# Attention from normalised rows: joined weights, and slice sums that are projected afterwards

## The chip, the cores and the metric

The kernel runs on one core of a Trainium2 chip. The metric is device time in microseconds (us) of one execution; the time before is the median of three timed runs. A trace of one further, profiled execution gives all times of single instructions.

## The reference

The input is x, 4 images of 32 x 32 tokens with 128 channels. Three stages follow one another: a deformable convolution on group-normalised x, an attention over 32 learned slices for each of 8 heads, and a mixture of 8 experts (top 2). The change touches the attention alone:

```
def _L1_attn_ref(x, W_x, b_x, W_slice, b_slice, W_temp, b_temp, W_out, b_out):   # x: layer-normalised tokens
    x_proj = (x @ W_x.T + b_x).reshape(B, N, H, D).transpose(0, 2, 1, 3)         # B 4, N 1024, H 8, D 32
    adaptive_temp = BASE_TEMP + jnp.clip(x_proj @ W_temp.T + b_temp, -0.4, 0.4)
    slice_logits = x_proj @ W_slice.T + b_slice - log_neg_log_eps
    slice_weights = jax.nn.softmax(slice_logits / adaptive_temp, axis=2)         # over the tokens
    slice_norm = slice_weights.sum(axis=2)
    eidetic = jnp.einsum('bhnc,bhng->bhgc', x_proj, slice_weights)
    eidetic = eidetic / (slice_norm + 1e-05)[..., None]
    out_x = jnp.einsum('bhgc,bhng->bhnc', eidetic, slice_weights)
    return out_x.transpose(0, 2, 1, 3).reshape(B, N, H * D) @ W_out.T + b_out
```

## The kernel before

All arithmetic is in float32. The work of the convolution sets the beat: each of the 4 images has 8 groups of 10 slots, so 80 slots an image, and each engine runs one long program, slot after slot. In a slot TensorE makes one part of the products of interpolation weights (`products`, L872); behind slot 0 of each group it contracts the previous group's products with the values (`contract`, L888) and projects an older one (`project`, L896). VectorE makes distances and ramps (L1574, L1588) and copies products out of PSUM in even slots (`take`, L1597); ScalarE makes edges and ramps (L1259, L1265), copies products in most odd slots (`lift`, L1283) and copies the contraction's result (L1274); GpSimd weighs (L752, L763). `contract` waits until the products of all ten slots have been copied. All queues are in order, so an instruction that waits holds up all that stands behind it on its engine.

Attention, routing and the experts of image b are woven into the slots of the images behind it: `side(b, slot)` runs, ahead of a slot's own products, the steps that the tables `PE_STEPS`, `ACT_STEPS` and `DVE_STEPS` give for that slot, for image b-1, and for image b-2 those 80 slots later. The three woven images 0, 1 and 2 share PSUM banks 6 and 7 and one set of buffers, so that a step waits until the one before it has been copied out. The last image, 3, goes through the same steps in a tail behind the convolution, three slots ahead, with banks of its own; between its steps stand the expert tiles of image 2 (`tile`, L1124 and L1136, with a gelu on ScalarE, L1350), also by slot. GpSimd gathers the experts' rows of images 0 and 1 with 16 indirect transfers (L734) in slots 9 to 20 of the convolution two images later; VectorE adds them (`add_rows`, L1847) in slots 21 to 25.

The attention of one image, with the slots of before: the normalised rows are transposed (`turn_tn`, 9) and copied (`tnT`). They are projected twice: channels by tokens (`xpT0`, `xpT1`, 10 and 11; ScalarE adds the bias while copying, L1297) and tokens by channels (`xp0`, `xp1`, 13 and 15; VectorE adds the bias, L1647). The temperatures are a product of the former (`temps`, 12; VectorE clamps them, L1637 and L1639, and takes reciprocals in two halves, L1641 and L1643). Four steps `logits0` to `logits3` (18 to 21) make a block-diagonal product (L1024), spread the reciprocals over the heads' rows (L1025), add the bias on ScalarE (L1305) and multiply on VectorE (L1656); `max0`, `max1` and `exp0`, `exp1` follow for each half. The weights are transposed (`turn_e0`, `turn_e1`, 23 and 25) and copied (`e0`, `e1`, L1312), the sums over tokens taken against the second projection (`sums`, 26, L1042), masked (`bdE`, L1673), multiplied by the output weights (`M`, 27) and applied (`out`, 28, L1055).

## Time and profile before

| what | us |
|---|---|
| median of 3 timed runs | 1352.8 |
| lowest and highest | 1348.93, 1356.17 |
| the profiled execution | 1359.09 |
| its span, first to last instruction | 1357.0 |
| TensorE, VectorE, ScalarE, GpSimd busy | 1027.2, 834.3, 786.9, 676.2 |
| mean granted TensorE clock, as a share of full speed | 0.878 |

The busy times are those of the profiled execution. They overlap, and each is spread over three parts of the span: a short preparation, the convolution with the work woven into it (from about 53 to 1150 us), and the tail.

### The profile page before, as it was taken

The page shows a single profiled execution, that of the slowest core. Times are in us where ns is not written, and L with a number is a line of the kernel's source. Part 1 is how long each engine was busy: PE and PEld are TensorE (multiplying, and loading weights), DVE is VectorE, ACT ScalarE, POOL GpSimd, SP SyncE. Part 2 cuts the span into 40 slices and gives each one's busy share as a digit, 9 for nine tenths or more (in the row PEclk, how much of TensorE's full clock was granted, in tenths as well). Part 3 has the DMA queues.
Part 4 walks back from the last instruction along what each step waited for, and adds up shares of the span by engine and source line. Part 5 has one row for each costly group of instructions (what it writes and reads, how often), then busy time and mean ns, then how long its engine had stood idle before and what let it go on. Part 6 is the DMA issues. An engine that isn't in the chain of part 4 may idle for free.

```text
span 1357.0 us, 51003 instructions
## 1 busy us (share of the span) xinstructions
PE 1027.2 (76%) x22444; PEld 838.1 (62%) x22444; DVE 834.3 (61%) x1632; ACT 786.9 (58%) x1435; POOL 676.2 (50%) x640
## 2 busy tenths in 40 slices
PE   4576877886887758998787758988777678768790
PEld 3455655565566646886576647875566466558690
DVE  5767766676648846556678645566678474535361
ACT  2786756765667644667567545766675542354460
POOL 2664545554535593435745764437655852002334
PEclk9697987978989778999998778999997789886995
DMA  7302121311000322552110323632113120523612
GB/s 163 100 24 54 65 54 48 71 44 45 23 23 24 91 70 72 164 163 59 46 38 24 103 81 85 190 102 57 39 37 89 45 68 25 165 78 93 193 54 75
DMA packets 140445, 103.26 MB, mean 76 GB/s; under 512 B 43529, under 2 KB 123714, under 8 KB 139714
## 3 DMA queue, kind: packets, MB, share of 16 engines
q1 hardware_dynamic: 136130, 91.61, 24.5%
q0 software_dynamic: 4096, 8.40, 2.1%
q8 instruction: 179, 2.93, 0.9%
q14 instruction: 40, 0.33, 0.1%
HBM read 76.31 MB, written 23.66 MB: 74 GB/s over the span
## 4 chain that ended last, share of the span: by engine, by line
PE 55%; ACT 19%; DVE 14%; issue 7%; DMA 2%; POOL 1%; SPq 1%; DVEq 0%; POOLq 0%; ACTq 0%
PE ps L888 13%; PE ps L872 10%; ACT xsb L1265 7%; PE ps L1124 6%; PE ps L896 6%; PE ps L1136 5%; DVE asb L1597 3%; ACT asb L1283 2%; ACT xsb L1259 2%; DMA ring<-in_L_ffn_W 2%; DVE region L1820 2%; PE ps L845 2%; DVE xsb L1574 2%; PE ps L1042 1%; DVE ysb L1588 1%
## 5 line engine op out<-in xcount | busy, mean ns | idle before, releaser
L763 POOL TENSOR_TENSOR ysb<-ysb,rw 128x576 f32<-128x576 f32 x300 | 336.8, 1145 | 366.5 <-DVE ysb L1588 366.3
L872 PE MATMUL ps<-xsb,ysb 64*64 64x96 f32 x11008 | 331.1, 272 | 111.0 <-DVE asb L1597 27.0
L872 PEld LDWEIGHTS ps<-xsb,ysb 64*64 64x64 f32 x11008 | 281.6, 151 | 174.0 <-issue 78.5
L1265 ACT ACTIVATE xsb<-xsb,pick 128x576 f32<-128x576 f32 (+1 forms) x480 | 336.2, 750 | 5.2
L1597 DVE COPY asb<-ps 128x960 f32<-128x960 f32 (+1 forms) x208 | 215.7, 1043 | 112.3 <-PE ps L888 100.0
L752 POOL TENSOR_TENSOR ysb<-rw,count 128x576 f32<-128x576 f32 (+1 forms) x150 | 174.3, 1162 | 78.3 <-PE ps L872 77.4
L888 PE MATMUL ps<-asb,vd 32*32 32x258 f32 x8192 | 183.0, 388 | 18.8 <-issue 16.6
L1274 ACT ACTIVATE osp<-ps 128x258 f32<-128x258 f32 x128 | 43.0, 443 | 254.2 <-PE ps L888 254.2
L1350 ACT ACTIVATE region<-ps,b_col 128x128 f32<-128x128 f32 x368 | 105.3, 370 | 103.6 <-PE ps L1124 101.8
L888 PEld LDWEIGHTS ps<-asb,vd 32*32 32x32 f32 x8192 | 121.5, 103 | 69.1 <-issue 35.9
L1574 DVE TENSOR_TENSOR xsb<-rw,ps 128x576 f32<-128x576 f32 (+1 forms) x150 | 108.4, 722 | 60.8 <-PE ps L872 59.9
L1588 DVE SCALAR_TENSOR_TENSOR ysb<-ysb,ps 128x576 f32<-128x576 f32 (+1 forms) x158 | 113.7, 719 | 20.1 <-POOL ysb L752 20.1
L724 POOL DMA_INDIRECT sorted_rows<-region,row_no x64 | 63.5, 993 | 122.1 <-DVE row_no L1785 105.5
L1259 ACT ACTIVATE xsb<-xsb 128x576 f32<-128x576 f32 (+1 forms) x160 | 105.3, 658 | 23.5 <-DVE xsb L1574 23.5
L1124 PE MATMUL ps<-region,ring 128*128 128x128 f32 x552 | 88.1, 308 | 26.8 <-ACT region L1350 11.2
L1283 ACT ACTIVATE asb<-ps 128x768 f32<-128x768 f32 x112 | 93.8, 837 | 24.9 <-PE ps L872 24.7
L1124 PEld LDWEIGHTS ps<-region,ring 128*128 128x128 f32 x552 | 75.8, 212 | 38.4 <-issue 22.9
L734 POOL DMA_INDIRECT picked<-expert_rows,row_no x64 | 63.1, 986 | 59.3 <-DMA expert_rows<-xsb 24.6
L896 PE MATMUL ps<-outw,osp 128*128 128x128 f32 x512 | 78.6, 317 | 11.9 <-issue 7.8
L1606 DVE TENSOR_TENSOR x_tok<-x_tok,ps 128x1024 f32<-128x1024 f32 x32 | 39.0, 1218 | 75.0 <-PE ps L896 71.7
L896 PEld LDWEIGHTS ps<-outw,osp 128*128 128x128 f32 x512 | 72.5, 226 | 17.6 <-issue 14.0
L1136 PE MATMUL ps<-ring,region 128*128 128x128 f32 x552 | 78.2, 288 | 6.0 <-ACT region L1350 4.0
(270 smaller groups left out, 1220.2 us busy)
## 6 DMA issues: line engine op xcount, KB each, us to landing
ring<-in_L_ffn_W SPq DMA_DIRECT2D x138, 256.0 KB, 3.2
vd<-group_values SPq DMA_DIRECT2D x128, 128.0 KB, 2.7
set_rows<-ring SPq DMA_DIRECT2D x4, 1376.0 KB, 6.6
rw<-set_rows SPq DMA_DIRECT2D x30, 172.0 KB, 3.4
group_values<-region SPq DMA_DIRECT2D x32, 128.0 KB, 3.6
asb<-in_L_ffn_W SPq DMA_DIRECT2D x16, 256.0 KB, 4.8
region<-sorted_rows SPq DMA_DIRECT2D x6, 512.0 KB, 4.9
expert_rows<-region SPq DMA_DIRECT2D x6, 512.0 KB, 5.3
```

What stands on the lines that cost most here:

```text
L752: pl.tensor_tensor(ysb[:, ch % DEPTH, 0:sets, NU - 1, :], rows_of(ig)[:, 1, first:first + sets].rearrange("p (s o) -> p s o", o=1) .broadc ...
L763: pl.tensor_tensor(ysb[:, ch % DEPTH, 0:sets, u, :], ysb[:, ch % DEPTH, 0:sets, NU - 1, :], rows_of(ig)[:, 2 + u, first:first + sets].rear ...
L872: last = pe.matmul(ps[64 * j:64 * j + 64, bank + i, NV * GRID * q:NV * GRID * (q + 1)], ysb[rows, ch % DEPTH, col, :, :].rearrange("p u y ...
L888: last = pe.matmul(ps[32 * jc:32 * jc + 32, j, 0:NI * AM], vd[rows, ig % 2, x, :], asb[rows, x, :, :].rearrange("p i n -> p (i n)"), start ...
L896: last = pe.matmul(pcol(project_bank(ig), t), osp[:, ig % 2, t // 4, t // 2 % 2, t % 2 * P:(t % 2 + 1) * P], outw[:, ig % G, :], start=Tru ...
L1124: last = pe.matmul(ps[:, hidden_bank(b, i), j * P:(j + 1) * P], ring_part(b, i, 0)[:, j * P:(j + 1) * P], turned_rows(b, i), start=True, s ...
L1136: last = pe.matmul(ps[:, expert_bank(b, i), 0:C], hT[:, i % 2, j, :], ring_part(b, i, 1)[:, j * P:(j + 1) * P], start=(j == 0), stop=(j == ...
L1259: act.activation(away, away, ACT.Relu, bias=1.0, scale=-1.0).then_inc(s.x_within, 1)
L1265: act.activation(xsb[:, ch % DEPTH, 0:sets, v, :], xsb[:, ch % DEPTH, 0:sets, NV - 1, :], ACT.Relu, bias=pick[:, v:v + 1], scale=-1.0).the ...
L1574: dve.tensor_tensor(xsb[:, ch % DEPTH, 0:sets, NV - 1, :], rows_of(ig)[:, 0, first:first + sets].rearrange("p (s o) -> p s o", o=1) .broad ...
L1588: dve.scalar_tensor_tensor(v, v, 0.0, units.rearrange("p (o q) -> p o q", o=1) .broadcast_to([P, sets, GRID]), ALU.max, ALU.min).then_inc( ...
L1597: dve.tensor_copy(asb[:, :, :, first:first + m].rearrange("p x i m -> p i x m"), ps[:, bank:bank + 2, 0:GRID * m].rearrange("p i (m x) -> ...
```

## The change

The two projections of the rows fall away. In their place two products of weights are made once, in slot 12 of image 0's convolution (`join_weights`): `wc`, the projection times the block-diagonal slice weights, and `wtc`, the projection times the temperature weights; the biases are carried through likewise. Temperatures and logits are taken from the transposed normalised rows `tnT` with these. The sums are taken of the normalised rows themselves (all 256 columns against 128 channels), copied to SBUF by ScalarE, and projected afterwards in a new step `eid`; the bias enters there as `bx_b` times a diagonal matrix of the sums of weights, which VectorE makes (`diagonal`). The tables of steps are renumbered: `temps` from 12 to 11, `logits0` to `logits3` from 18 to 21 to 16 to 19, the transposes from 23 and 25 to 21 and 23, `sums` to 25, `eid` at 26; `M` and all that follows stay where they were. The diff's core, first TensorE, then ScalarE (`join_weights`, `sums`), then VectorE (`xp0` to `bdE`):

```
+PE_STEPS = {9: ("turn_tn",), 11: ("temps",), 16: ("logits0",), 17: ("logits1",), 18: ("logits2",), 19: ("logits3",),
+            21: ("turn_e0",), 23: ("turn_e1",), 25: ("sums",), 26: ("eid",), 27: ("M",), 28: ("out",),
...
             def join_weights():
+                pe.wait_ge(s.setup_done, 1)
+                pe.wait_ge(s.turned_copied, 2)
+                pe.wait_ge(s.ln_cols_copied, 4)
+                temp_columns = wt_bd.rearrange("p (m f) -> p m f", f=HG)[:, :, 0]
+                for h in range(2):
+                    pe.matmul(ps[:, 6, h * P:(h + 1) * P], wx_raw[:, h, :], ws_bd, start=True, stop=True)
+                for h in range(2):
+                    pe.matmul(ps[:, 6, 2 * P + h * DH:2 * P + (h + 1) * DH], wx_raw[:, h, :], temp_columns,
+                              start=True, stop=True)
+                pe.matmul(ps[:, 7, 0:2], ws_bd, bx_col[:, :], start=True, stop=True)
+                for i in range(4):
+                    last = pe.matmul(ps[32 * i:32 * i + 32, 7, 2:3], temp_columns, bx_col[:, i // 2:i // 2 + 1],
+                                     start=True, stop=True)
+                last.then_inc(s.weights_joined, 1)
...
-                elif step in ("xpT0", "xpT1"):
...
+                elif step == "temps":
                     pe.wait_ge(s.tnT_copied, b + 1)
-                    for c in range(2):
-                        last = pe.matmul(ps[:, bank_of(b, 1 + h) + c, :], wxT[:, h * P:(h + 1) * P],
-                                         tnT[:, c * 512:(c + 1) * 512], start=True, stop=True)
...
+                        last = pe.matmul(ps[32 * i:32 * i + 32, bank_of(b, 3), :], wtc[:, h * DH:(h + 1) * DH],
+                                         tnT[:, c * 512:(c + 1) * 512], start=True, stop=True)
                     last.then_inc(s.temps_summed, 1)
-                elif step in ("xp0", "xp1"):
...
-                    pe.matmul(ps[:, bank, :], ws_bd[:, :], xpT[:, h, c * 512:(c + 1) * 512], start=True, stop=True)
+                    pe.matmul(ps[:, bank, :], wc[:, h * P:(h + 1) * P], tnT[:, c * 512:(c + 1) * 512],
+                              start=True, stop=True)
...
                 elif step == "sums":
                     pe.wait_ge(s.e_copied, 2 * b + 2)
+                    for t in range(NT):
+                        last = pe.matmul(ps[:, bank_of(b, 12), 0:2 * P], tn_tok[:, t, :], own(b).e_tok[:, t, :],
+                                         start=(t == 0), stop=(t == NT - 1))
+                    last.then_inc(s.slice_sums, 1)
+                elif step == "eid":
+                    pe.wait_ge(s.diagonal_made, b + 1)
+                    pe.wait_ge(s.sums_copied, b + 1)
                     for h in range(2):
-                        for t in range(NT):
-                            last = pe.matmul(ps[:, bank_of(b, 12), h * P:(h + 1) * P], own(b).xp_tok[:, t, h * P:(h + 1) * P],
-                                             own(b).e_tok[:, t, h * P:(h + 1) * P], start=(t == 0), stop=(t == NT - 1))
-                    last.then_inc(s.slice_sums, 1)
+                        both = ps[:, bank_of(b, 12) + 1, h * P:(h + 1) * P]
+                        pe.matmul(both, bx_b[:, h * P:(h + 1) * P], own(b).diagonal[:, h, :], start=True, stop=False)
+                        last = pe.matmul(both, wxT[:, h * P:(h + 1) * P], own(b).sums[:, h, :], start=False, stop=True)
+                    last.then_inc(s.eid_summed, 1)
...
+            def join_weights():
+                act.wait_ge(s.weights_joined, 1)
+                act.activation(wc[:, :], ps[:, 6, 0:2 * P], ACT.Copy).then_inc(s.joined_copied, 1)
+                act.activation(wtc[:, :], ps[:, 6, 2 * P:2 * P + 2 * DH], ACT.Copy).then_inc(s.joined_copied, 1)
...
+                elif step == "sums":
+                    act.wait_ge(s.slice_sums, b + 1)
+                    act.activation(own(b).sums, ps[:, bank_of(b, 12), 0:2 * P].rearrange("p (h n) -> p h n", h=2),
+                                   ACT.Copy).then_inc(s.sums_copied, 1)
...
-                elif step in ("xp0", "xp1"):
...
+                elif step == "diagonal":
+                    dve.wait_ge(s.exp_done, 2 * b + 2)
+                    for h in range(2):
+                        last = dve.tensor_scalar(own(b).diagonal[:, h, :], ident[:, :], a_sum[:, h:h + 1], None, ALU.mult)
+                    last.then_inc(s.diagonal_made, 1)
...
                 elif step == "bdE":
-                    dve.wait_ge(s.slice_sums, b + 1)
+                    dve.wait_ge(s.eid_summed, b + 1)
```

How this stands on TensorE for the first woven image, from slot 9 to slot 19. In these rows L872 (after: L892) are products, L888 (L908) the contraction, L986 and L1005 before the two projections, L993 (L1005) the temperatures, L1024 and L1025 (L1018 and L1020) one step of the logits. Before:

```order
L978 MATMUL ps<-ident,region 128x128 x8
L872 MATMUL ps<-xsb,ysb 64x96 x16
L986 MATMUL ps<-region,wxT 128x512 x2
L872 MATMUL ps<-xsb,ysb 64x96 x20
L888 MATMUL ps<-asb,vd 32x258 x128
L986 MATMUL ps<-region,wxT 128x512 x2
L872 MATMUL ps<-xsb,ysb 64x96 x16
L993 MATMUL ps<-region,wt_bd 32x512 x4
L872 MATMUL ps<-xsb,ysb 64x96 x20
L1005 MATMUL ps<-wxT,region 128x256 x4
L872 MATMUL ps<-xsb,ysb 64x96 x36
L1005 MATMUL ps<-wxT,region 128x256 x4
```

And after, the same stretch:

```order
L999 MATMUL ps<-ident,region 128x128 x8
L892 MATMUL ps<-xsb,ysb 64x96 x36
L908 MATMUL ps<-asb,vd 32x258 x128
L1005 MATMUL ps<-region,wtc 32x512 x4
L892 MATMUL ps<-xsb,ysb 64x96 x88
L1018 MATMUL ps<-region,wc 128x512
L1020 MATMUL ps<-region,head_pick 128x512
L892 MATMUL ps<-xsb,ysb 64x96 x16
L1018 MATMUL ps<-region,wc 128x512
L1020 MATMUL ps<-region,head_pick 128x512
```

Nothing stands between the products of slots 9 and 10 and the contraction any more, the temperatures come right behind the contraction, and the logits start in slot 16 with only products between.

On ScalarE, around slot 19 of the same image: L1305 (after: L1309) adds the logits' bias, L1341 (L1349) is the exponential with its table load, L1283 (L1292) `lift`, L1274 before the copy of the contraction's result, L1265 (L1274) ramps. Before:

```order
L1283 ACTIVATE asb<-ps 128x2x32x12
L1305 ACTIVATE region<-ps,bslice_col 128x512
L1259 ACTIVATE xsb<-xsb 128x18x32
L1265 ACTIVATE xsb<-xsb,pick 128x18x32
L1274 ACTIVATE osp<-ps 128x2x43x3 x4
L1305 ACTIVATE region<-ps,bslice_col 128x512
L1341 ACT_TABLE_LOAD
L1341 ACTIVATE region,a_sum<-region,a_nmax 128x1024
```

And after:

```order
L1309 ACTIVATE region<-ps,bslice_col 128x512
L1349 ACT_TABLE_LOAD
L1349 ACTIVATE region,a_sum<-region,a_nmax 128x1024
L1274 ACTIVATE xsb<-xsb,pick 128x18x32 x2
L1292 ACTIVATE asb<-ps 128x2x32x12
L1268 ACTIVATE xsb<-xsb 128x18x32
L1274 ACTIVATE xsb<-xsb,pick 128x18x32
L1283 ACTIVATE osp<-ps 128x2x43x3 x4
```

The first exponential stood behind the contraction of slot 20 and the copy of its result; it now stands ahead of the copy of slot 19's products, for which that contraction waits.

In the tail, on TensorE, L1124 and L1136 (after: L1126 and L1138) are the expert tiles of image 2 between the steps of image 3; L1036 (L1031) are the transposed weights, L1042 (L1036) the sums, L1048 (L1050) is M. Before:

```order
L1036 MATMUL ps<-ident,xsb 128x128 x16
L1124 MATMUL ps<-region,ring 128x128 x4
L1136 MATMUL ps<-ring,region 128x128 x4
L1042 MATMUL ps<-xsb 128x128 x16
L1048 MATMUL ps<-woutT,ysb 128x128 x2
```

And after:

```order
L1031 MATMUL ps<-ident,xsb 128x128 x8
L1126 MATMUL ps<-region,ring 128x128 x4
L1138 MATMUL ps<-ring,region 128x128 x4
L1031 MATMUL ps<-ident,xsb 128x128 x8
L1036 MATMUL ps<-xsb,region 128x256 x8
L1126 MATMUL ps<-region,ring 128x128 x4
L1138 MATMUL ps<-ring,region 128x128 x4
L1044 MATMUL ps<-ysb,bx_b 128x128
L1045 MATMUL ps<-ysb,wxT 128x128
L1044 MATMUL ps<-ysb,bx_b 128x128
L1045 MATMUL ps<-ysb,wxT 128x128
L1050 MATMUL ps<-woutT,ysb 128x128 x2
```

One tile has moved between the two transposes, and one from ahead of the sums to behind them, where it stands ahead of the new step.

## Rows read from the trace of the kernel before

**Rows 1.** The page: busy time, costliest groups (busy, mean ns | idle before, releaser).

```profile
PE 1027.2 (76%) x22444; PEld 838.1 (62%) x22444; DVE 834.3 (61%) x1632; ACT 786.9 (58%) x1435; POOL 676.2 (50%) x640
...
L1265 ACT ACTIVATE xsb<-xsb,pick 128x576 f32<-128x576 f32 (+1 forms) x480 | 336.2, 750 | 5.2
...
L1588 DVE SCALAR_TENSOR_TENSOR ysb<-ysb,ps 128x576 f32<-128x576 f32 (+1 forms) x158 | 113.7, 719 | 20.1 <-POOL ysb L752 20.1
```

**Rows 2.** Groups by line, the projections and their copies, over all images.

```profile
L1005 PE MATMUL ps<-wxT,region 128*128 128x256 f32 x64 | 16.8, 408 | 5.7 <-DVE region L1647 5.7
...
L986 PE MATMUL ps<-region,wxT 128*128 128x512 f32 x32 | 16.6, 643 | 1.7 <-ACT region L1293 1.7
...
L1297 ACT ACTIVATE region<-ps,bx_col 128x1024 f32<-128x1024 f32 x8 | 8.9, 1115 | 7.0 <-PE ps L986 7.0
...
L1647 DVE TENSOR_TENSOR region<-ps,bx_b 128x1024 f32<-128x1024 f32 x6 | 7.0, 1160 | 0.0
```

**Rows 3.** Windows: stretch, length, busy by engine, granted clock, DMA.

```profile
338.40:370.20 31.80, 27.69 (x640) 16.95 (x640) 21.28 (x27) 20.70 (x32) 19.11 (x18) 0.97 0.09 25
370.20:410.80 40.60, 33.40 (x720) 26.40 (x724) 18.97 (x29) 26.61 (x42) 14.70 (x14) 0.92 0.07 19
410.80:437.60 26.80, 20.04 (x640) 16.61 (x629) 22.35 (x87) 20.36 (x33) 14.73 (x14) 0.94 0.11 30
...
397.46:403.21 5.75, 5.75 (x36) 5.63 (x39) 0.00 (x0) 3.24 (x5) 0.00 (x0) 0.65 0.00 0
1204.07:1207.81 3.74, 3.73 (x34) 3.54 (x32) 0.29 (x1) 0.69 (x3) 0.00 (x0) 1.00 0.50 134
```

**Rows 4.** Timeline of image 0's attention, TensorE: start, us, line, [idle before <-releaser].

```profile
338.32 2.83 PE L986 MATMUL ps<-region,wxT 128*128 128x512 f32 x4
...
363.52 1.10 PE L1024 MATMUL ps<-region,ws_bd 128*128 128x512 f32 x2 [1.02 <-DVE region L1647]
...
367.17 1.12 PE L1024 MATMUL ps<-region,ws_bd 128*128 128x512 f32 x2 [0.68 <-DVE region L1656]
...
374.57 2.02 PE L896 MATMUL ps<-outw,osp 128*128 128x128 f32 x16 [0.56 <-issue]
...
382.45 1.13 PE L1024 MATMUL ps<-region,ws_bd 128*128 128x512 f32 x2
...
397.46 5.75 PE L1042 MATMUL ps<-region 128*128 128x128 f32 x32 [1.80 <-ACT region L1312]
...
405.43 3.84 PE L1055 MATMUL ps<-region 128*128 128x128 f32 x32
```

**Rows 5.** Timeline of image 0's attention, VectorE and ScalarE.

```profile
347.80 1.16 DVE L1597 COPY asb<-ps 128x960 f32<-128x960 f32 x1 [4.25 <-PE ps L888]
...
351.98 0.75 DVE L1637 TENSOR_SCALAR region<-ps,btemp_col 128x512 f32<-128x512 f32 x1 [3.02 <-PE ps L993]
...
355.50 1.74 DVE L1641 RECIPROCAL region<-region 128x256 f32<-128x256 f32 x1
...
371.30 0.83 ACT L1283 ACTIVATE asb<-ps 128x768 f32<-128x768 f32 x1
...
385.38 1.28 ACT L1341 ACT_TABLE_LOAD   x1
```

**Rows 6.** Timeline of image 2's attention, GpSimd and VectorE.

```profile
934.75 2.06 POOL L763 TENSOR_TENSOR ysb<-ysb,rw 128x512 f32<-128x512 f32 x2 [3.00 <-DVE ysb L1588]
...
967.62 0.88 DVE L1847 SCALAR_TENSOR_TENSOR x_tok<-picked,g_w,x_tok 128x128 f32<-128x128 f32 x3 [3.32 <-DMA picked<-expert_rows,row_no]
...
983.30 0.42 DVE L1673 TENSOR_TENSOR region<-ps,head_mask 128x256 f32<-128x256 f32 x1 [0.33 <-PE ps L1042]
```

**Rows 7.** The chain that ended last, in the tail: start, us, what.

```profile
1164.99 1.98 PE ps L986 x4
...
1180.00 0.86 PE ps L1024 x2
...
1204.23 3.59 PE ps L1042 x32
```

More of the change, by code:

```diff
@@ L263, in conv_attn_moe @@
         osp = sb("osp", [P, 2, NI, NU, NJ * AM])
-        REGION = 11776
+        REGION = 11680
         region = sb("region", [P, REGION])
@@ L306, in conv_attn_moe, with slices @@
         tnT = part(N)
-        xpT = part(2 * N).rearrange("p (h n) -> p h n", h=2)
-        Slices = namedtuple("Slices", "temp rtemp xp_tok eT e_tok bdE Msb")
-        def slices(temp, rtemp, xp_tok, eT, e_tok, bdE, Msb):
-            return Slices(temp, rtemp, xp_tok.rearrange("p (t c) -> p t c", t=NT),
-                          eT.rearrange("p (h n) -> p h n", h=2), e_tok.rearrange("p (t c) -> p t c", t=NT),
-                          bdE.rearrange("p (h n) -> p h n", h=2), Msb.rearrange("p (h n) -> p h n", h=2))
-        woven_slices = slices(part(512), part(512), part(NT * 256), part(2 * N), part(NT * 256), part(2 * P), part(2 * P))
+        Slices = namedtuple("Slices", "temp rtemp eT e_tok bdE Msb sums diagonal")
+        def slices(temp, rtemp, eT, e_tok, *quads):
+            return Slices(temp, rtemp, eT.rearrange("p (h n) -> p h n", h=2), e_tok.rearrange("p (t c) -> p t c", t=NT),
+                          *(quad.rearrange("p (h n) -> p h n", h=2) for quad in quads))
+        woven_slices = slices(part(512), part(512), part(2 * N), part(NT * 256), *(part(2 * P) for _ in range(4)))
         x_flat = xsb[:, :, :, :, :].rearrange("p d s v x -> p (d s v x)")
@@ L318, in conv_attn_moe @@
         last_slices = slices(y_flat[:, 0:512], y_flat[:, 512:1024], x_flat[:, 0:2 * N], x_flat[:, 2 * N:4 * N],
-                             x_flat[:, 4 * N:6 * N], y_flat[:, 1024:1024 + 2 * P], y_flat[:, 1024 + 2 * P:1024 + 4 * P])
+                             *(y_flat[:, 1024 + 2 * P * i:1024 + 2 * P * (i + 1)] for i in range(4)))
         def own(b):
@@ L955, in wait_for_banks @@
                         pe.wait_ge(s.ln_cols_copied, 4)
+                    if slot > JOIN_SLOT:
+                        pe.wait_ge(s.joined_copied, 2)
+                        pe.wait_ge(s.biases_joined, 1)
                     return
@@ L1159, in side @@
                         turn_weights()
+                    if slot == JOIN_SLOT:
+                        join_weights()
                 for b_, at in (works(b, slot) if b < B else tail_works(slot)):
@@ L1293, in attend @@
                     act.activation(tnT, two(bank_of(b, 0)), ACT.Copy).then_inc(s.tnT_copied, 1)
-                elif step in ("xpT0", "xpT1"):
-                    h = int(step[-1])
-                    act.wait_ge(s.xpT_summed, 2 * b + h + 1)
-                    act.activation(xpT[:, h, :], two(bank_of(b, 1 + h)), ACT.Identity, bias=bx_col[:, h:h + 1])\
-                       .then_inc(s.xpT_copied, 1)
                 elif step[:-1] == "logits":
@@ L1366, in side @@
                         turn_weights()
+                    if slot == JOIN_SLOT:
+                        join_weights()
                 for b_, at in (works(b, slot) if b < B else tail_works(slot)):
@@ L1643, in attend @@
                     dve.reciprocal(own(b).rtemp[:, 256:512], own(b).temp[:, 256:512]).then_inc(s.rtemp_ready, 1)
-                elif step in ("xp0", "xp1"):
-                    half = int(step[-1])
-                    dve.wait_ge(s.xp_summed, 2 * b + half + 1)
-                    dve.tensor_tensor(own(b).xp_tok[:, 4 * half:4 * half + 4, :],
-                                      two(bank_of(b, 4 + half)).rearrange("p (t c) -> p t c", t=4),
-                                      bx_b[:, :].rearrange("p (o c) -> p o c", o=1).broadcast_to([P, 4, 256]),
-                                      ALU.add).then_inc(s.xp_copied, 1)
                 elif step[:-1] == "logits":
@@ L1871, in side @@
                         turn_weights()
+                    if slot == JOIN_SLOT:
+                        join_weights()
                 for b_, at in (works(b, slot) if b < B else tail_works(slot)):
```

92 lines of the change are left out of this document (37 added, 55 removed), and 2 rows, old and new, of the table DVE_STEPS.

## The prediction, before the changed kernel was run

> **What bounds the kernel now.** I read the page first: TensorE is busy for 76% of the span, VectorE for 61%, ScalarE for 58%, GpSimd for 50% [rows 1]. No engine is full, and the shares are averages over stages with different limits, so the next view is the one by stretches. Image 0's attention is woven into slots 10 to 29 of image 1's convolution. Those twenty slots take 31.8 and 40.6 us, the ten slots behind them 26.8 us with TensorE busy for 20.0 us [rows 3]. So each woven attention stretches the loop, by about 72.4 - 2 x 26.8 = 19 us, and the change can win back a part of that 19 three times. For the fourth image nothing is woven: its attention runs alone in the tail, and the chain goes through it step by step [rows 7].
>
> Then I read the timelines of the two places for waits. In image 0 TensorE stands still ahead of logits, transposes and sums for 0.7 to 1.8 us at a time, each time for VectorE or ScalarE [rows 4]. In image 2 a further engine shows: GpSimd issues 16 row gathers in slots 9 to 20. Its last wait is the 3.00 us at 934.75, and behind it its instructions stand end to end until the last gather has gone out; VectorE then waits 3.32 us for the gathered rows at 967.62 [rows 6]. Image 1 has the same gathers, image 0 has none.
>
> **What is removed from TensorE.** The two products that project the rows cost 16.6 and 16.8 us over four images [rows 2]: 8.35 us an image. The slice sums keep their columns (16 matmuls of 128 become 8 of 256), so I leave them at the 3.74 us that the tail shows at full clock [rows 3]. The four new matmuls of 128 columns ("eid") are a quarter of that: 0.9 us. Net 7.4 us an image, 30 us in all. ScalarE loses two copies of 1.1 us and gains one of 256 columns (about 0.45, estimated from the 1.1 us for 1024 [rows 2]). VectorE loses two additions of 1.16 us [rows 2] and gains two small ones ("diagonal", about 0.25 us each, a 128-column share of the same row, rounded up). None of this is the gain yet: that depends on what each place waits for next.
>
> **Image 0, slots 10 to 20.** The first projection stands between the products of slots 9 and 10 and takes 2.83 us [rows 4]. Without it the contraction behind slot 10 starts 1.8 us earlier (the products themselves run at the slower clock there for that time). Its end, which VectorE's copy at 347.80 waited for [rows 5], moves to 345.9; temperatures follow at once. On VectorE that copy takes until 347.1; then come two clamps (0.75 for the first [rows 5], 1.2 in all), the first reciprocal (1.74 [rows 5]), this slot's own distance, ramp (0.72 [rows 1]) and copy, 2.5 together, and the second reciprocal: 354.3. Logits start there instead of at 363.52 [rows 4]: 9.2 us earlier. But they come in four slots in a row, at the 3.65 us from one to the next that rows 4 show, so the last ends at 354.3 + 3 x 3.7 + 2.1 = 367.5. **What is late next** is the contraction of slot 20. It waits for ScalarE's copy of slot 19's products, which before stood at 371.30 ahead of the exponential, and now stands behind the last biasing (0.69), the table load (1.28 [rows 5]), the exponential (1.34 with the reading of its sum) and two ramps (0.75 each [rows 1]), and takes 0.83 itself: 367.5 + 5.7 = 373.2. Before, it started behind the projection of 374.57, at 376.6 [rows 4]. So of 9.2 us **3.4 us** are left.
>
> **Image 0, slots 21 to 29.** From the end of that contraction to the output product it was 405.43 - 382.45 = 23.0 us [rows 4]. In the new order: transpose 1.1, copy 1.0, exponential 1.35, second transpose from +3.8 to +4.9, its copy behind a chunk's edges and ramps until +8.4, sums to +12.2, their copy and eid to +14.0, mask and products, M, output at +16.5. That is **6.5 us** less: logits 3 with its 2.2 us is gone from here, and so is most of the waiting (1.80 us ahead of the sums alone [rows 4]), while 1.4 us for the copy and eid are new. Two of the 6.5 us are clock: the sums took 5.75 us here at a granted clock of 0.65, 3.74 us in the tail at 1.00 [rows 3]. Image 0 together 10 us; bounds 5 (sums and output at the lower level) and 13 (the wait of slot 20 doesn't appear).
>
> **Images 1 and 2.** The same moves, but GpSimd has to have issued its gathers. By the working above the ramp that it waits for at 934.75 comes 2 us earlier, at 932.7 (the first reciprocal now stands ahead of it). GpSimd then runs end to end as before, so VectorE's adding of gathered rows starts at 965.6 instead of 967.62. From there to the mask of the sums VectorE needed 983.30 - 967.62 = 15.7 us [rows 6]; logits 3 and the maximum behind it (2.1) have moved ahead, the diagonals (0.5) come in: 14.1, and the mask stands at 979.7, **about 4 us** earlier. TensorE is done with eid by 974 and now waits for that mask: here the wait on logits goes, and one on VectorE comes. I give images 1 and 2 4 us each; bounds 1 (GpSimd isn't moved at all and VectorE's gain is eaten by its shared waits) and 8.
>
> **The tail.** Before, the chain runs through both projections from 1164.99, to logits at 1180.00 and the sums at 1204.23 [rows 7]. Expert tiles of image 2 stand between the steps, at places fixed by the slot. In the new order temperatures start behind the pair of tile 2 at 1165.9, both reciprocals are through at 1172.2, and logits start 7.7 us earlier. The tile of slot 16 (2.0 us) now comes behind logits 0, not ahead, and the one of slot 22 between the transposes, where its gelu and the table load for it delay a copy by about 1 us. The sums start 8.5 us earlier; behind them stand the tile of slot 25 (2.0) and eid (0.9) ahead of the mask. Left: **5.5 us**, bounds 3 and 9. All that follows (routing, sorting, image 3's experts) hangs on this chain and moves with it.
>
> **Set-up.** Nine small matmuls in slot 12 of the first convolution, two small copies, two small VectorE instructions. At the 0.23 us of a 128-column matmul (3.74 / 16 [rows 3]) nine are at most 2.1 us, and the copies are partly covered by slot 12's products: **+2 us**, bounds 1 and 3.
>
> **Sum.** -10 - 4 - 4 - 5.5 + 2 = -21.5 us. The profiled execution took 1359.1 us (span 1357.0), 0.5% over the median of the three timed runs, 1352.8. So 1359.1 becomes 1337.6, a ratio of 0.984, and on the median 1331.5 us. All bounds together give -7 and -37.
>
> **Rivals.**
> *The gathers hide it.* If GpSimd's queue sets images 1 and 2 completely, only image 0, the tail and the set-up count: -10 - 5.5 + 2 = -13.5, 1339 us. For it: the unbroken stretch behind 934.75. Against: from 967.62 on it is VectorE that is late, and it loses 2.1 us of work there [rows 6].
> *No new waits.* The wait of slot 20 and the one for the mask turn out short, every bound falls on the good side: -37, 1316 us. For it: a plain group takes 26.8 us [rows 3], so there is room.
> *Slower: the clock.* With logits in a row TensorE idles for about 2 us ahead of them and about 5 ahead of M. If this costs it the higher level (2.4 GHz) from slot 16 to slot 28, the four logits pairs (2.1 us each) and what stands in slots 21 to 28 (11 us) take twice their time: +19 us an image, against gains of 10, 4 and 4. That ends at about +35 us, 1387 us; the sign turns once some 7 us of TensorE's work an image run at the lower level (1.2 GHz) that do not now. For it: the sums of image 0 ran partly at that level, behind a stretch with waits [rows 3, 4]. Against: the plain group has TensorE busy for 20.0 of 26.8 us, 75%, at a clock of 0.94, and the woven groups keep about 80% by my working (now 87% and 82% at 0.97 and 0.92 [rows 3]).
> The Trainium skill, TensorE: Matmul & The Clock Gate, section "What's actually happening", speaks against this change: the throttled level is the default there, and activity is what releases it, so that work taken from TensorE can be paid for in clock. By that rule alone the time would be nearer to that rival's; the trace shows both levels, but not at this busy share.
>
> **How the numbers follow.** My forecast, 13 to 30 us less, gets 0.60; the gathers hiding it (7 to 13 us less) 0.15; no new waits (over 30 less) 0.13; a clock that eats most of the gain, within 0.5%, 0.07; the slower clock case 0.05. 0.5% is 6.8 us, about what a measurement here can tell from no change. So faster 0.88, the same 0.07, slower 0.05. The range runs from 1317 (-36 us) to 1343 (-10): it leaves out the clock cases and a sliver at each end.
>
> **What would show it.** In the profile after: the twenty woven slots of image 0 near 62 us instead of 72.4; logits about 3.7 us apart in slots 16 to 19; the contraction of slot 20 waiting for ScalarE's copy; in images 1 and 2 TensorE waiting about 5 us ahead of M for VectorE; the tail's sums 8 us earlier against its start, its mask 5.5. I am wrong if the granted clock of slots 16 to 28 falls under 0.85, if the wait of slot 20 is over 6 us, or if the woven slots of images 1 and 2 don't shorten.

## The result and the profile after

The changed kernel took 1333.3 us (median of 4 runs, 1331.8 to 1335.9), the kernel before 1354.5 us beside it: a ratio of 0.985, interval 0.981 to 0.989. The forecast was 1331.5 us. The total came out as forecast; several of its terms did not.

The page of the kernel after, its first line (us, share of the span, instructions); it answers to [rows 1]:

```profile
PE 989.9 (74%) x22334; PEld 808.8 (61%) x22334; DVE 825.9 (62%) x1633; ACT 778.2 (58%) x1433; POOL 676.9 (51%) x640
```

TensorE is busy for 37 us less; the removed products, counted at full clock, were 30. The rest is clock, and it is not shown to belong to the change: in the second profiles told below TensorE is busy for 1029.1 us before and 1009.9 us after, only 19 us less.

Windows of the kernel after, columns as in [rows 3]: image 0's slots 10 to 19, then 20 to 29, then the part of the first in which the logits start:

```profile
333.51:368.10 34.59, 29.08 (x635) 16.52 (x635) 22.53 (x29) 19.49 (x32) 19.06 (x18) 0.83 0.08 23
368.10:400.51 32.41, 27.91 (x703) 23.21 (x699) 17.45 (x27) 25.51 (x41) 14.76 (x14) 1.00 0.09 24
348.80:359.85 11.05, 10.35 (x73) 4.50 (x73) 7.43 (x9) 5.11 (x8) 7.54 (x8) 0.54 0.07 17
```

Together 67.0 us in place of 72.4 [rows 3], where the forecast named 62. The second half gained. The first got longer, although it lost the projections and took in only two of the logits steps. The third row says why: TensorE has work for 10.35 of 11.05 us there, at a granted clock of 0.54. The timeline of TensorE in that stretch, kernel after (L892 products, L1018 and L1020 one logits step, L908 the contraction):

```profile
349.38 1.56 PE L892 MATMUL ps<-xsb,ysb 64*64 64x96 f32 x32 [2.71 <-DVE asb L1610]
351.04 2.07 PE L1018 MATMUL ps<-region,wc 128*128 128x512 f32 x2
353.05 2.07 PE L1020 MATMUL ps<-region,head_pick 32*128 32x512 f32 x2
...
365.10 1.13 PE L1018 MATMUL ps<-region,wc 128*128 128x512 f32 x2 [0.68 <-DVE region L1662]
...
372.76 3.84 PE L908 MATMUL ps<-asb,vd 32*32 32x258 f32 x172 [1.86 <-ACT asb L1292]
```

TensorE waits 2.71 us for a copy that stands on VectorE behind the two clamps and the first reciprocal; then the same instruction takes 2.07 us that takes 1.13 three slots later. VectorE ahead of that copy (L1650 and L1652 the clamps, L1654 the reciprocal, L1610 the copy), and below it the second clamp in the kernel before:

```profile
343.26 0.74 DVE L1650 TENSOR_SCALAR region<-ps,btemp_col 128x512 f32<-128x512 f32 x1
344.03 1.30 DVE L1652 TENSOR_SCALAR region<-region 128x512 f32<-128x512 f32 x1
345.37 1.75 DVE L1654 RECIPROCAL region<-region 128x256 f32<-128x256 f32 x1
...
348.18 1.15 DVE L1610 COPY asb<-ps 128x960 f32<-128x960 f32 x1
```

```profile
352.76 0.43 DVE L1639 TENSOR_SCALAR region<-region 128x512 f32<-128x512 f32 x1
```

The last row of TensorE's timeline is a wait that the prediction named: slot 20's contraction for ScalarE's copy, 1.86 us.

Image 2 in the kernel after, TensorE (L1050 is M, L1057 the output), to be held against [rows 4, 6]:

```profile
960.13 1.22 PE L1050 MATMUL ps<-woutT,region 128*128 128x128 f32 x4 [2.87 <-DVE region L1684]
961.28 1.56 PE L892 MATMUL ps<-xsb,ysb 64*64 64x96 f32 x32
962.77 5.64 PE L1057 MATMUL ps<-region 128*128 128x128 f32 x32
```

and VectorE ahead of it (L1858 adds gathered rows, L1684 is the mask):

```profile
946.02 1.66 DVE L1858 SCALAR_TENSOR_TENSOR x_tok<-picked,g_w,x_tok 128x128 f32<-128x128 f32 x6 [1.62 <-DMA picked<-expert_rows,row_no]
...
955.86 2.81 DVE L1858 SCALAR_TENSOR_TENSOR x_tok<-picked,g_w,x_tok 128x128 f32<-128x128 f32 x4
...
959.65 0.42 DVE L1684 TENSOR_TENSOR region<-ps,head_mask 128x256 f32<-128x256 f32 x1
```

The wait ahead of M is the forecast one, at 2.87 us of about 5 (4.39 in image 1). Not forecast is what follows it: the output takes 5.64 us, where it took 3.84 us in image 0 before [rows 4] and in image 2 before:

```profile
985.48 3.84 PE L1055 MATMUL ps<-region 128*128 128x128 f32 x32
```

The mask starts 13.6 us behind VectorE's first add (946.02 to 959.65), and that add waits for the gathered rows. Image 1 has the same 13.6 us:

```profile
660.50 1.67 DVE L1858 SCALAR_TENSOR_TENSOR x_tok<-picked,g_w,x_tok 128x128 f32<-128x128 f32 x6 [3.13 <-DMA picked<-expert_rows,row_no]
...
674.13 0.42 DVE L1684 TENSOR_TENSOR region<-ps,head_mask 128x256 f32<-128x256 f32 x1
```

The tail of the kernel after, TensorE; its steps answer to [rows 7], L1036 are the sums, L1126 and L1138 a tile:

```profile
1146.18 1.12 PE L1018 MATMUL ps<-region,wc 128*128 128x512 f32 x2 [2.94 <-DVE ysb L1656]
1147.23 1.86 PE L1020 MATMUL ps<-ysb,head_pick 32*128 32x512 f32 x2
1149.02 2.08 PE L1126 MATMUL ps<-region,ring 128*128 128x128 f32 x8
...
1172.37 6.59 PE L1036 MATMUL ps<-xsb,region 128*128 128x256 f32 x16 [2.28 <-ACT xsb L1316]
```

Twice the same picture: a wait of 2 to 3 us, and soon behind it work at the lower level. The sums take 6.59 us, where before they took 3.74 [rows 3].

### The profile page after: what moved, and what is told of

Its sections match the earlier page's. It is cut to its first block, busy times and chain, and to the rows that moved or that the text cites. A ratio compares the mean times of both kernels' runs of the same rounds, so it can differ in the third digit from the quotient of the medians.

```text
span 1331.2 us, 50787 instructions
## 1 busy us (share of the span) xinstructions
PE 989.9 (74%) x22334; PEld 808.8 (61%) x22334; DVE 825.9 (62%) x1633; ACT 778.2 (58%) x1433; POOL 676.9 (51%) x640
## 3 DMA queue, kind: packets, MB, share of 16 engines
q1 hardware_dynamic: 136130, 91.61, 24.7%
## 4 chain that ended last, share of the span: by engine, by line
PE 50%; ACT 19%; DVE 16%; issue 8%; POOL 3%; DMA 3%; SPq 1%; DVEq 0%; POOLq 0%; ACTq 0%
PE ps L908 13%; PE ps L892 9%; ACT xsb L1274 7%; PE ps L1126 6%; PE ps L1138 5%; PE ps L916 5%; DVE asb L1610 4%; ACT asb L1292 2%; DMA ring<-in_L_ffn_W 2%; ACT xsb L1268 2%; POOL picked L737 2%; DVE region L1831 2%; PE ps L848 2%; DVE ysb L1601 2%; DVE xsb L1587 2%
## 5 line engine op out<-in xcount | busy, mean ns | idle before, releaser
L892 PE MATMUL ps<-xsb,ysb 64*64 64x96 f32 x11008 | 323.5, 267 | 124.3 <-DVE asb L1610 32.1
L892 PEld LDWEIGHTS ps<-xsb,ysb 64*64 64x64 f32 x11008 | 274.7, 147 | 183.2 <-issue 84.6
L1274 ACT ACTIVATE xsb<-xsb,pick 128x576 f32<-128x576 f32 (+1 forms) x480 | 336.7, 751 | 5.2
L1610 DVE COPY asb<-ps 128x960 f32<-128x960 f32 (+1 forms) x208 | 215.7, 1043 | 120.3 <-PE ps L908 109.5
L755 POOL TENSOR_TENSOR ysb<-rw,count 128x576 f32<-128x576 f32 (+1 forms) x150 | 175.1, 1167 | 70.7 <-PE ps L892 70.1
L908 PE MATMUL ps<-asb,vd 32*32 32x258 f32 x8192 | 184.2, 391 | 28.6 <-issue 18.8
L1283 ACT ACTIVATE osp<-ps 128x258 f32<-128x258 f32 x128 | 43.0, 443 | 246.8 <-PE ps L908 246.8
L908 PEld LDWEIGHTS ps<-asb,vd 32*32 32x32 f32 x8192 | 124.1, 103 | 78.2 <-issue 46.4
L1126 PE MATMUL ps<-region,ring 128*128 128x128 f32 x552 | 85.5, 302 | 28.2 <-ACT region L1358 13.1
L1292 ACT ACTIVATE asb<-ps 128x768 f32<-128x768 f32 x112 | 93.8, 838 | 12.8 <-PE ps L892 12.7
L1126 PEld LDWEIGHTS ps<-region,ring 128*128 128x128 f32 x552 | 72.9, 205 | 41.1 <-issue 26.0
L737 POOL DMA_INDIRECT picked<-expert_rows,row_no x64 | 62.9, 983 | 62.2 <-DMA expert_rows<-xsb 25.9
L1138 PE MATMUL ps<-ring,region 128*128 128x128 f32 x552 | 77.5, 286 | 6.0 <-ACT region L1358 4.0
L916 PEld LDWEIGHTS ps<-outw,osp 128*128 128x128 f32 x512 | 70.3, 220 | 15.4 <-issue 11.3
```

The costliest lines, as they stand in the source:

```text
L755: pl.tensor_tensor(ysb[:, ch % DEPTH, 0:sets, NU - 1, :], rows_of(ig)[:, 1, first:first + sets].rearrange("p (s o) -> p s o", o=1) .broadc ...
L892: last = pe.matmul(ps[64 * j:64 * j + 64, bank + i, NV * GRID * q:NV * GRID * (q + 1)], ysb[rows, ch % DEPTH, col, :, :].rearrange("p u y ...
L908: last = pe.matmul(ps[32 * jc:32 * jc + 32, j, 0:NI * AM], vd[rows, ig % 2, x, :], asb[rows, x, :, :].rearrange("p i n -> p (i n)"), start ...
L916: last = pe.matmul(pcol(project_bank(ig), t), osp[:, ig % 2, t // 4, t // 2 % 2, t % 2 * P:(t % 2 + 1) * P], outw[:, ig % G, :], start=Tru ...
L1126: last = pe.matmul(ps[:, hidden_bank(b, i), j * P:(j + 1) * P], ring_part(b, i, 0)[:, j * P:(j + 1) * P], turned_rows(b, i), start=True, s ...
L1138: last = pe.matmul(ps[:, expert_bank(b, i), 0:C], hT[:, i % 2, j, :], ring_part(b, i, 1)[:, j * P:(j + 1) * P], start=(j == 0), stop=(j == ...
```

## The experiments

This table holds, for every profiled run, the length of seven stretches in us, from the end of one slot's products on TensorE to that of another (slots 10 to 21, which hold slot 20's contraction and, before and in the old slots, logits 3 as well; slots 22 to 29; the tail from the last products to the end of the span), and the median of the timed runs. Behind it stands the ratio to the kernel before, timed beside it: the runs were taken in rounds, and the kernel before took 1357.7 us in one, 1350.9 and 1354.6 in the others, so totals of different rounds are compared by this ratio alone. "Adds", "exp", "tail" and "woven" are the edits told below.

| kernel | image 0: 10-21, 22-29 | image 1 | image 2 | tail | median (runs), ratio |
|---|---|---|---|---|---|
| before | 47.1, 25.3 | 49.2, 25.0 | 47.2, 25.0 | 217.0 | 1354.5 (4) |
| before again | 47.5, 25.1 | 49.6, 23.5 | 49.1, 25.0 | 216.6 | 1352.4 (1) |
| after | 47.8, 19.2 | 44.1, 25.9 | 47.9, 24.9 | 216.9 | 1333.3 (4), 0.985 |
| after again | 45.8, 19.2 | 44.7, 24.7 | 49.2, 21.0 | 213.8 | 1335.2 (6), 0.985 |
| old slots | 44.0, 26.7 | 48.0, 26.6 | 44.4, 26.0 | 207.0 | 1341.9 (6), 0.989 |
| tail in old slots | 49.9, 19.2 | 50.0, 23.4 | 49.8, 21.1 | 206.3 | 1333.5 (6), 0.987 |
| tail kept busy | 45.9, 19.2 | 44.8, 26.0 | 44.1, 26.6 | 209.5 | 1329.2 (6), 0.986 |
| woven kept busy | 44.3, 19.0 | 45.8, 26.4 | 43.7, 26.7 | 213.1 | 1331.4 (6), 0.981 |
| exp behind lift | 48.8, 19.2 | 42.1, 26.3 | 44.9, 26.3 | 214.2 | 1332.2 (6), 0.984 |
| adds later | 47.1, 19.2 | 44.2, 19.2 | 47.7, 19.2 | 214.1 | 1328.4 (6), 0.981 |
| adds later, tail in old slots | 53.3, 19.2 | 45.2, 19.2 | 49.8, 19.2 | 210.6 | 1329.1 (6), 0.982 |
| three edits | 43.7, 19.2 | 48.5, 19.2 | 44.6, 19.2 | 209.4 | 1323.0 (6), 0.974 |
| four edits | 42.9, 19.2 | 41.7, 19.2 | 42.1, 19.2 | 205.4 | 1318.1 (6), 0.974 |

**Both kernels again, unedited.**

> The changed kernel once more, nothing edited, to see which stretches of its profile repeat. Theory 1 (what the first profile showed is the change): 1333 us within 3; the ten slots 20 to 29 of image 0 take 32.4 us again, image 2's 39.5, the sums of the tail 6.6 us at the lower clock, each within 0.5 us. Theory 2 (much of the stretch-by-stretch difference is where the granted clock happens to fall): the total is again within 3 us of 1333, but some of these stretches move by 2 us or more against each other, among them groups of slots in which the change touches nothing.

> The kernel before once more, nothing edited, for a second profile of it. Theory 1 (the stretches that the first profile gave are the kernel's own): the ten slots 40 to 49 of images 0, 1 and 2 take 34.5, 34.1 and 34.8 us again, slots 20 to 29 of image 0 take 40.6, each within 0.5 us, and the tail 217. Theory 2 (part of them is where the granted clock fell in that one execution): at least two of these move by 2 us or more, the total stays within 8 us of 1354.

Theory 2 for the changed kernel: the total came back at 1335.2 us, but the tail's sums took 3.7 us this time, slots 22 to 29 of image 2 took 21.0 us instead of 24.9, and slots 40 to 49 of images 1 and 2, where the change touches nothing, 2.1 and 1.5 us more. The kernel before repeats better: its three groups of slots 40 to 49 came within 0.5 us, its image 0 too; slots 0 to 9 of image 1's convolution moved by 4.3 us. So a single stretch of one profile is good to some 4 us, and a verdict has to rest on a stretch that returns in several kernels.

**The new arithmetic in the old slots.** TensorE's table; those of ScalarE and VectorE are changed alike.

```
-PE_STEPS = {9: ("turn_tn",), 11: ("temps",), 16: ("logits0",), 17: ("logits1",), 18: ("logits2",), 19: ("logits3",),
-            21: ("turn_e0",), 23: ("turn_e1",), 25: ("sums",), 26: ("eid",), 27: ("M",), 28: ("out",),
+PE_STEPS = {9: ("turn_tn",), 12: ("temps",), 18: ("logits0",), 19: ("logits1",), 20: ("logits2",), 21: ("logits3",),
+            23: ("turn_e0",), 25: ("turn_e1",), 26: ("sums", "eid"), 27: ("M",), 28: ("out",),
```

> The new arithmetic in the old kernel's slots: temperatures in slot 12, reciprocals in 13 and 15, logits in 18 to 21, exponentials in 21 and 23, transposes in 23 and 25, sums and their projection in 26. Nothing is left out. Theory 1 (it is the removed work that gives the time: two projections and two biased copies per image fewer): within 4 us of the changed kernel, 1330 to 1337. Theory 2 (half of it is the steps standing two slots earlier, which keeps the mask and the last product from being waited for in slots 25 to 28): 1340 to 1346, with image 0's slots 20 to 29 at 36 to 39 us in place of 32.

1341.9 us, 0.989 of before (0.983 to 0.994), 16 us less than the kernel before beside it (1357.7), where the changed kernel's second turn took 22 less (0.985, 0.981 to 0.989). The two intervals overlap, so the totals do not settle what the earlier slots add. In the woven slots the arithmetic alone gives little: image 0's twenty take 70.7 us against 72.4 and 72.6, image 1's 74.6 against 74.3 and 73.1, image 2's 70.4 against 72.2 and 74.1. The steps standing earlier are worth some 5 us in images 0 and 1 (67.0 and 65.0, 70.0 and 69.4 us in the new slots), nothing in image 2 (72.8 and 70.3). Theory 2 holds for the total; the stretch that it named, image 0's slots 20 to 29, took 42.0 us and not 36 to 39. In the tail it is the other way round: 207.0 us, 10 less than before, where the new slots gained 0 to 3. The four logits steps of the tail and a tile between them, kernel in the old slots (window, columns as in [rows 3]):

```profile
1156.90:1166.20 9.30, 9.30 (x32) 3.98 (x32) 3.64 (x6) 3.23 (x8) 0.00 (x0) 1.00 0.34 113
```

That is the higher level throughout; in the kernel after, the stretch from 1146.00 to 1160.30 has a granted clock of 0.76. In the old slots a tile more stands between temperatures and logits, and TensorE waits 0.43 us for the reciprocals instead of 2.94.

**The last image alone in the old slots**, images 0 to 2 in the new ones: each engine takes its steps for image 3 from the table above.

> The changed kernel, with the steps of the last image alone in the slots of the kernel before; images 0, 1 and 2 keep the new ones. Nothing is left out. Theory 1 (in the tail the earlier slots leave TensorE 2.9 us without work ahead of the logits, which then run at the lower clock, 12.5 us from the first to the last instead of 9.2; the tiles that stood there filled it): the tail falls from 214 to 217 us to 206 to 209, the total to 1325 to 1329. Theory 2 (the tail ends with the transfers and the gathers, whatever the logits do, or the lower clock falls on another stretch of the tail instead): within 2 us of the changed kernel.

The tail is at 206.3 us, as theory 1 has it. The total is not: 1333.5 us (1329.4 to 1339.1). The profile shows the rest: the woven slots 10 to 29 took 69.1, 73.5 and 70.9 us in it, 2 to 4 us more than in the kernel after for images 0 and 1, in code that is the same. The gain in the tail is shown, one in the total is not.

**TensorE kept busy in the tail's waits.** The helper, and the last of the places where it is called.

```
+            def keep_busy(b, use, times):
+                for _ in range(times):
+                    pe.matmul(ps[:, bank_of(b, use), :], wc[:, 0:P], tnT[:, 0:512], start=True, stop=True)
...
                 elif step == "sums":
+                    if not woven:
+                        keep_busy(b, 12, 2)
                     pe.wait_ge(s.e_copied, 2 * b + 2)
```

> The changed kernel with six extra products of 128 by 512 in the tail, whose sums nobody reads, while TensorE waits there: two ahead of the first logits, one ahead of each set of transposes of the exponentials, two ahead of the slice sums. Theory 1 (the lower clock of the logits and of the sums follows from TensorE's waits just before them): the logits take 9.2 us in place of 12.5, the sums 3.6 to 3.8, the granted clock there is 1.00, and the total is 1326 to 1330. Theory 2 (the clock falls there anyway, or falls a little later): the stretch keeps a mean clock of 0.75 and the total is 1333 to 1337, since the extra products then cost up to 4 us.

1329.2 us; the tail takes 209.5. The ratio, 0.986, is no lower than the changed kernel's 0.985, so a gain in the total is not shown. The sums in this kernel (timeline, L1048) and the tile behind the first logits:

```profile
1147.97 2.07 PE L1138 MATMUL ps<-region,ring 128*128 128x128 f32 x8
...
1170.21 3.72 PE L1048 MATMUL ps<-xsb,region 128*128 128x256 f32 x16 [0.56 <-ACT xsb L1328]
```

The sums are at the higher level, but the edit is not shown to be the reason: they took 3.7 us in the four other profiles of the unedited new tail too, and 6.59 us stands alone. The logits take 10.8 us, from the end of their first product to that of the last, instead of 12.5, with a tile still at the lower level: 1.22 us of the wait ahead of the logits were left. So here theory 1 holds for part of the stretch. All four logits steps ran at the higher level in the last run below, which has the same six products, and in the three profiles with the tail in the old slots, in none of the five with the unedited new tail.

**TensorE kept busy in the woven waits.** One product of the same kind in slot 13 and one in slot 15.

```
-PE_STEPS = {9: ("turn_tn",), 11: ("temps",), 16: ("logits0",), ...
+PE_STEPS = {9: ("turn_tn",), 11: ("temps",), 13: ("busy",), 15: ("busy",), 16: ("logits0",), ...
...
+                elif step == "busy":
+                    if woven:
+                        pe.wait_ge(s.scale_chain, 2 * b + 1)
+                        keep_busy(b, 6, 1)
```

> The changed kernel with two extra products of 128 by 512 for each of images 0, 1 and 2, one in slot 13 and one in slot 15, whose sums nobody reads: there TensorE waits 2.7 to 3 us behind VectorE's reciprocals. Theory 1 (the logits of slots 16 to 19 run at the lower clock because of that wait): slots 15 to 19 show a granted clock of 0.95 or more, slots 10 to 19 of image 0 take 30 to 32 us where seven profiles of these slots gave 33.3 to 40.9, and the total is 1326 to 1331. Theory 2 (the clock is low there for what came before, or the extra products take TensorE's time from the convolution): these slots keep their spread of 33 to 41 us and the total is 1334 to 1341.

The test of the clock. Image 0 in this kernel, timeline (L991 the extra product, L1026 and L1028 the first logits step), then the window of slots 15 to 19:

```profile
351.75 1.13 PE L991 MATMUL ps<-region,wc 128*128 128x512 f32 x2
353.77 0.89 PE L892 MATMUL ps<-xsb,ysb 64*64 64x96 f32 x32 [0.90 <-DVE asb L1618]
355.43 1.12 PE L1026 MATMUL ps<-region,wc 128*128 128x512 f32 x2 [0.77 <-DVE region L1664]
356.48 1.12 PE L1028 MATMUL ps<-region,head_pick 32*128 32x512 f32 x2
```

```profile
351.82:369.45 17.63, 13.93 (x188) 6.28 (x192) 13.71 (x19) 12.01 (x19) 11.36 (x11) 1.00 0.04 12
```

The same slots in the kernel after, and when it ran again:

```profile
346.68:368.10 21.42, 17.24 (x187) 7.97 (x191) 14.56 (x20) 12.78 (x21) 11.40 (x11) 0.76 0.04 10
```

```profile
351.86:371.15 19.29, 14.43 (x188) 6.82 (x190) 14.48 (x20) 12.78 (x21) 11.37 (x11) 0.91 0.04 11
```

More work for TensorE, and the stretch is 1.7 to 3.8 us shorter. One of the extra products stands ahead of it, in slot 13; slots 10 to 19 with both take 32.1 us, against 34.6 and 33.3. Nobody reads the extra sums and no other engine has a different instruction, so what they change is when TensorE stands still, and with it the clock. In image 0 the wait of 2.7 us stands ahead of the logits in all eight profiles of the new slots without the extra products, and the clock fell in all eight; in the two with them the longest wait there is 0.9 us, and it stayed. Logits now run at 1.00 in all three images, here and in the last run below; without the extra products that held in 7 of 16 cases for image 1 or 2, in none for image 0. Images 1 and 2 as a whole win nothing clear by it here (72.2 and 70.4 us for the twenty slots), since they wait for the mask afterwards (slots 22 to 29 take 26.4 and 26.7 us). The total, 1331.4 us, is inside the range of the unedited kernel's runs.

**The exponential behind the copy.**

```
-ACT_STEPS = {... 19: ("logits3", "exp0"), ...
+ACT_STEPS = {... 19: ("logits3",), 20: ("exp0",), ...
```

> The changed kernel with the first exponential moved on ScalarE from slot 19 to slot 20, so that the copy of slot 19's taken values stands ahead of the table load and the exponential. Theory 1 (the contraction in slot 20 waits for that copy): image 0 wins 2.5 to 3.5 us in slots 19 to 21 and the total falls by 2.5 to 6 us, to 1327 to 1331, if images 1 and 2 wait there too. Theory 2 (in images 1 and 2 other waits end last, and in image 0 the wait only moves to the transposes in slot 21): within 1.5 us of the changed kernel.

The contraction of image 0 in this kernel, timeline; its predecessor ends at 371.84:

```profile
369.79 2.05 PE L916 MATMUL ps<-outw,osp 128*128 128x128 f32 x16
371.77 3.87 PE L908 MATMUL ps<-asb,vd 32*32 32x258 f32 x172
```

The 1.86 us of waiting are gone, and slots 10 to 21 of images 1 and 2 are 2.3 and 3.7 us shorter than the mean of the two profiles of the changed kernel. But slots 22 to 29 are 1.0 and 3.3 us longer, as theory 2 has it for these images: the mask ends last, and TensorE waits 5.27 us for it ahead of M in both, where it waited 4.39 and 2.87. Image 2:

```profile
960.44 1.22 PE L1050 MATMUL ps<-woutT,region 128*128 128x128 f32 x4 [5.27 <-DVE region L1684]
```

Image 0 as a whole doesn't show the gain, since more of its logits ran at the lower level in this profile. By the total, 1332.2 us, the two kernels can't be told apart.

**The adds later.**

```
-ADD_SLOT, ADD_SLOTS = 101, 5
+ADD_SLOT, ADD_SLOTS = 110, 5
```

> The changed kernel with the adding of the gathered rows of the image before moved on VectorE from slots 21 to 25 to slots 30 to 34, behind the mask and the last product. Theory 1 (in images 1 and 2 the mask stands on VectorE behind these adds, TensorE waits some 3 us for it and comes back at the lower clock): slots 20 to 29 of image 2 fall from 39.5 to 34 to 36 us, the wait ahead of M below 1 us, image 1's likewise; total 1323 to 1328. Theory 2 (the adds only move, and hold up the products of slots 30 to 34 by what they cost in 21 to 25; or the gathers' transfers, not VectorE, set that stretch): slots 30 to 39 longer by 3 us or more per image and the total within 2 us of the changed kernel.

M and the output of image 2 in this kernel, timeline:

```profile
951.74 0.71 PE L1050 MATMUL ps<-woutT,region 128*128 128x128 f32 x4
...
953.40 3.84 PE L1057 MATMUL ps<-region 128*128 128x128 f32 x32
```

No wait, and the higher level. Slots 22 to 29 now take 19.2 us in all three images, against 21.0 to 25.9 in images 1 and 2. Theory 2 is half right too: slots 30 to 39 took 31.3 and 31.6 us instead of 26.8 to 28.9, so most of it is paid back there. The total is 1328.4 us, with runs from 1321.6 to 1337.9; its interval overlaps the changed kernel's. With the tail in the old slots as well:

> The changed kernel with the gathered rows added in slots 30 to 34 and with the last image's steps in the old slots, both together. If the two gains lie in different stretches and add up: 1316 to 1323, images 1 and 2 as in the run with the later adds (slots 20 to 29 at 32 and 34 us), the tail at 206 to 209 us. If the earlier end of the convolution only makes the tail wait for something else (the transfers of the late image's weights): 1325 to 1329.

1329.1 us. Neither reading fits cleanly: the woven slots kept their gain, the tail took 210.6 us, and image 0 had its worst stretch of all, 72.5 us, with all four logits steps at the lower level.

**The edits together**: adds later, the exponential behind the copy and the six products in the tail; then also the two in slots 13 and 15.

> The changed kernel with the later adds (slots 30 to 34), the exponential behind the copy (slot 20) and the six extra products in the tail, all three. If the gains stand in different stretches and add up (some 7, 2 to 6 and 4 to 6 us): 1318 to 1324, with the contraction in slot 20 about 2 us shorter in each image, slots 27 and 28 of images 1 and 2 at 1.5 and 4.8 us, and the tail at 209 us. If a gain in one place comes back as a lower clock elsewhere: 1326 to 1331.

> The three edits of the other run and the two extra products in slots 13 and 15 of images 0, 1 and 2. If these keep the clock at its higher level in slots 15 to 19: 3 to 6 us less than with the three edits, 1314 to 1320. If they don't: the same as with the three edits or up to 6 us more.

1323.0 and 1318.1 us, both 0.974 of before (0.970 to 0.978), a per cent under the changed kernel alone and clear of its interval. Both totals lie in the range of the first reading of their expectations. Image 0 with four edits, windows as for the kernel after above:

```profile
337.23:370.13 32.90, 28.48 (x639) 16.98 (x638) 22.44 (x29) 19.52 (x32) 19.02 (x18) 0.88 0.08 24
370.13:399.34 29.21, 27.21 (x704) 22.91 (x699) 17.46 (x27) 25.50 (x41) 14.77 (x14) 1.00 0.09 27
```

All three woven images take 61 to 62 us, the forecast's number for image 0. Whether the fourth edit gives more on top is not settled by the totals: the intervals are the same.

## Why the total was right and its terms were not

Means of two profiles of each kernel; the spans differ by 23 us. Image 0 is divided where the prediction divides it, at the end of slot 20's contraction, and not as in the table.

- **Set-up**, +2: the ten slots that hold it went from 29.5 and 29.9 us to 32.3 and 31.2. Right.
- **Image 0, behind that contraction**, -6.5: to the end of slot 29 it went from 28.2 and 28.0 us to 21.0 in every profile with the new slots, -7.1. Right, with its reasons: logits 3 gone from there, the sums at the higher level.
- **Image 0, from slot 10 to that contraction**, -3.4: 44.1 and 44.6 us before, 46.0 and 44.0 after, +0.6. This is the mis-sized term. The order of events was right (earlier logits, then slot 20 late behind ScalarE's copy), but I took the logits to come at the 3.65 us a step of [rows 4], that is at the higher level. They came behind a wait of 2.7 us and began at the lower level, the second step 5.6 us and the third 4.8 us behind the one before it in the first profile. With that wait filled the stretch took 42.3 us, which is -2.1. The rest is a late start: the logits began 17.5 and 18.4 us behind the end of slot 9, where my working has 15.9. Slot 10's contraction ended 0.7 us earlier in one profile and 0.1 us later in the other, not 1.8 earlier, and the second clamp took 1.30 us where I had counted 0.45; why it did stays open.
- **Images 1 and 2**, -4 each: measured -4.0 and -1.7. The mask waited behind the adds as forecast and came 6.4 and 2.8 us earlier, counted from the end of slot 9; I priced the wait and not the 1.8 us that the output, and 0.5 and 0.7 us that M and the products of slot 27, lose behind it in image 2.
- **The tail**, -5.5: measured -1.5. The logits started 8 us earlier as worked out, the sums only 6 and not 8.5, and time was lost where the tiles no longer filled TensorE's waits. With the six extra products the tail gives 7 us, with the old slots 10 us.
- **Not in the sum**: these terms make -11.5 of the 23 us. The other half lies where no step was changed, 8.1 of it in slots 40 to 49 of images 0 to 2. In image 0 the same 16 products (L1094 before, L1096 after) took 3.77 us at the lower level before and 2.05 us after. It isn't reliable: all six such groups of before took 34.1 to 35.3 us, and of 33 in the eleven profiles with the new arithmetic 21 took 33.0 us or more, the others 30.7 to 32.0. Whether the change made it rarer, or the two profiles of the changed kernel were lucky, stays open; so does why.

So the total fell within 2 us of the forecast because three shortfalls, together 10 us, met a gain of the same size that I had not seen: so close a total was luck. One reading was off as well: TensorE's waits in image 0 before went up to 2.16 us, ahead of the second transposes, not 1.8. Of the rivals, the slower clock was the mechanism that took most of the shortfalls, at a fraction of the +19 us an image that I gave it; over slots 16 to 28 of the three images the granted clock was 0.92 to 0.98 in both profiles, above the 0.85 at which I had said I would be wrong, and low only in short parts. "The gathers hide it" was half right. In images 1 and 2 VectorE's first add waited for the gathered rows in 10 of 12 cases with the adds in their place and the new woven slots, the mask followed 13.6 to 14.4 us later, and with the exponential behind the copy what was won ahead of the mask was lost again in waiting for it. Against it, as the prediction had said, that stretch got shorter (15.7 us [rows 6]); and the queue holds these images only through the adds: with them later and GpSimd's instructions unchanged, slots 22 to 29 took the 19.2 us of image 0. "No new waits" named 1316 us; the four edits, which take away or fill those waits, come to 1318.

The Trainium skill, TensorE: Matmul & The Clock Gate, section "What's actually happening", says that throttled is the default and activity releases it. The runs with extra products agree: 2.25 us of useless work a woven image keeps slots 15 to 19 at 1.00.

## What to carry to other kernels

When work is taken out ahead of a step, look at what TensorE then does instead: if it stands still, price the work behind the wait at the lower clock too, and see whether steps from elsewhere, or even useless products, can stand in the gap. Before moving a step forward, look at who is queued on the engine that it will wait for; the adds behind which the mask stood took back, in images 1 and 2, what was won ahead of them. And take a second profile of the same kernel before you explain a stretch by the change.

## What the runs showed of the hardware that I had not expected

A wait of 2.71 us on TensorE was followed by 9.5 us at the lower level, although TensorE was busy for 9.40 of them (349.38 to 358.90, granted clock 0.50). Such a wait is not always followed by it: ahead of the tail's sums 2.28 us were, in the first profile, and 2.19 us were not, in the run with the exponential behind the copy (6.59 and 3.72 us for the same sums). And the same program varies: with identical instructions, of image 0's four logits steps between a part of the first and all four ran at the lower level in different profiles of the new slots, which moves slots 10 to 21 from 45.8 to 53.3 us, and whole runs of one kernel by up to 1.4% (1326.8 to 1345.6 us with the exponential behind the copy).
